# Natural context tiles loaded in three pieces of 112, 12 and 1 partitions in place of two of 112 and 13

## What is computed

```python
x = x + xattn(layernorm(x), ctx, ...)   # softmax(q k^T * scale) v, then a projection
x = x + ffn(layernorm(x), ...)          # L0: routed + shared experts, L1: 4 MoE layers, L2: top-2 experts, L3: quantised linear
```

## Time and profile before

| | us |
|---|---|
| median of 3 runs | 5644.4 |
| the runs | 5640.87, 5644.4, 5651.05 |
| profiled execution, its own time | 5660.02 |
| span in the profile | 5658.3 |

### The profile page before, as it was taken

How to read it: one execution, slowest core, us unless ns; L and a number is a source line. 1 busy time by engine, 2 the same in 40 slices (tenths; PEclk the granted TensorE clock), 3 DMA queues, 4 the chain that set the end, 5 groups by cost and what they waited for, 6 DMA issues and landing times. The chain is left out here.

```text
span 5658.3 us, 103574 instructions
## 1 busy us (share of the span) xinstructions
PE 4693.5 (83%) x32385; PEld 3818.4 (67%) x32385; DVE 3713.5 (66%) x7873; ACT 2780.5 (49%) x6184; POOL 2171.9 (38%) x1902
## 2 busy tenths in 40 slices
PE   5499999994699899899899847787799999996784
PEld 4366666663588888888888835665566666664574
DVE  4477777776566656656656546777677777775545
ACT  0277777773233333333333224455477777773341
POOL 0266666662311110110110024555466666662321
PEclk7699999996799999999999967888799999997887
DMA  7333443340100100100100020000344333420183
GB/s 244 76 83 83 89 88 86 81 88 15 38 17 21 24 20 20 24 20 20 25 20 20 4 60 0 0 0 0 72 94 88 86 82 86 89 64 23 26 180 64
DMA packets 190530, 314.67 MB, mean 56 GB/s; under 512 B 132372, under 2 KB 140870, under 8 KB 190406
## 3 DMA queue, kind: packets, MB, share of 16 engines
q1 hardware_dynamic: 186822, 294.71, 23.4%
q10 hardware_dynamic: 3584, 18.43, 0.8%
HBM read 146.07 MB, written 19.54 MB: 29 GB/s over the span
## 5 line engine op out<-in xcount | busy, mean ns | idle before, releaser
L486 POOL TENSOR_TENSOR a2m_prob_n<-a2m_prob,a2m_rec 128x500 f32<-128x500 f32 x672 | 666.6, 1020 | 377.7 <-DVE a2m_rec L671 297.1
L486 POOL TENSOR_TENSOR a0m_prob_n<-a0m_prob,a0m_rec 128x500 f32<-128x500 f32 x672 | 666.2, 1019 | 374.3 <-DVE a0m_rec L671 300.1
L1244 ACT ACTIVATE a1m_prob<-a1m_ps_s,a1m_neg_max 128x500 f32<-128x500 f32 x672 | 405.8, 675 | 557.4 <-DVE a1m_neg_max L1182 557.4
L1103 PE MATMUL a1m_ps_o<-a1m_cn,a1m_prob_t 125*128 125x97 f32 x5376 | 653.8, 280 | 0.2 <-issue 0.2
L1103 PEld LDWEIGHTS a1m_ps_o<-a1m_cn,a1m_prob_t 125*128 125x128 f32 x5376 | 641.8, 198 | 0.4 <-issue 0.4
L1033 POOL TENSOR_TENSOR a1m_cxt<-a1m_raw,g_zeros 98x1500 fp32r<-98x1500 f32 x32 | 86.8, 2711 | 1430.1 <-PE a1m_ps_s L1069 1386.2
L1179 DVE TENSOR_REDUCE a1m_bank_max<-a1m_ps_s 128x1 f32<-128x500 f32 x672 | 455.7, 679 | 145.6 <-PE a1m_ps_s L1069 144.3
L649 DVE TENSOR_REDUCE a2m_bank_max<-a2m_ps_s 128x1 f32<-128x500 f32 x672 | 416.7, 671 | 159.6 <-PE a2m_ps_s L522 159.0
L649 DVE TENSOR_REDUCE a0m_bank_max<-a0m_ps_s 128x1 f32<-128x500 f32 x672 | 416.4, 670 | 159.0 <-PE a0m_ps_s L522 158.4
L727 ACT ACTIVATE a2m_prob<-a2m_ps_s,a2m_neg_max 128x500 f32<-128x500 f32 x672 | 446.7, 676 | 60.2 <-DVE a2m_neg_max L651 55.8
L727 ACT ACTIVATE a0m_prob<-a0m_ps_s,a0m_neg_max 128x500 f32<-128x500 f32 x672 | 446.5, 676 | 60.0 <-DVE a0m_neg_max L651 55.7
(11 more groups left out here) (747 smaller groups left out, 10163.5 us busy)
## 6 DMA issues: line engine op xcount, KB each, us to landing
a0m_ks<-a0m_k_hi SPq DMA_DIRECT2D x256, 187.5 KB
a2m_ks<-a2m_k_hi SPq DMA_DIRECT2D x256, 187.5 KB
a0m_ks<-a0m_k_lo SPq DMA_DIRECT2D x128, 187.5 KB
a2m_ks<-a2m_k_lo SPq DMA_DIRECT2D x128, 187.5 KB
ctx_t<-cprep_tr ACTq DMA_DIRECT2D x32, 562.5 KB
a0m_raw<-ctx_t SPq DMA_DIRECT2D x32, 562.5 KB
a1m_raw<-ctx_t SPq DMA_DIRECT2D x32, 562.5 KB
a2m_raw<-ctx_t SPq DMA_DIRECT2D x32, 562.5 KB
```

The costliest lines, as they stand in the source:

```text
L486: pool.tensor_tensor(prob_n[:, s, at], prob[:, s, at], rec[:, s:s + 1].broadcast_to([P, BK]), ALU.mult).then_inc(scaled, 1)
L1103: m = pe.matmul(ps_o[at, 0:CO], prob_t[:, u % 2, t, at], cn[:, h, t, :], start=(t == 0), stop=(t == KT - 1))
L1244: act.activation(prob[:, s, k * BK:(k + 1) * BK], ps_s[:, k, 0:BK], ACT.Exp, bias=neg_max[:, s:s + 1]).then_inc(exped, 1)
```

## The change

`SPLIT` gets a third slice: the 13 partitions become 12 and 1. The three waits on the tile's semaphore follow the number of slices. Nothing else differs.

```diff
-SPLIT = (slice(0, 112), slice(112, NK))
+SPLIT = (slice(0, 112), slice(112, 124), slice(124, NK))
...
                 for h in range(2):
-                    pe.wait_ge(loaded[h], 32 * (i + 1))
+                    pe.wait_ge(loaded[h], 16 * len(SPLIT) * (i + 1))
...
                 for h in range(slots):
-                    sp.wait_ge(ctx_in[h], 32 * ng)
+                    sp.wait_ge(ctx_in[h], 16 * len(SPLIT) * ng)
                     sp.wait_ge(ctxt_in[h], 16 * ng)
...
                     for h in sequences(u) if first_of(u) else ():
-                        pe.wait_ge(ctx_in[h], 32 * (i + 1 + (u // nu)))
+                        pe.wait_ge(ctx_in[h], 16 * len(SPLIT) * (i + 1 + (u // nu)))
```

## The result

| | before | after |
|---|---|---|
| median, us (20 runs each) | 5643.74 | 5652.93 |
| lowest and highest run, us | 5636.28, 5651.05 | 5641.51, 5666.18 |
| span of the profiled execution, us | 5658.3 | 5640.5 |

The ratio of after to before is 1.0018, 95% interval 1.0011 to 1.0026: some 10 us slower, between 6 and 15 by the interval, and about the 0.2% up to which the prediction called it no change.

A forecast was written before the change was run, and what follows sets the result against it. Prediction: TensorE is busy about 90% of the attentions; transfers set the pace in cprep, `raw` loads delay attention 3. Terms 0 + 2 + 0 + 1.2 = +3.2 us on the 5644.4 median gave 5648, range 5637 to 5663.

The forecast's parts named there:

- Issue in cprep, costed at nothing: cprep: the added issue ends 1.0 us after the first, within the 2 us of 7 rows per engine; cost 0.
- the price for lost cover as 16 us: cprep: if the 7 rows did not cover the added issue, 32 x 0.5 = 16 us.
- TensorE's wait for the tile: cprep: a sign to look for, this wait up by as much as the stage lengthens, 0 to 9 us.
- The lone row's engine in cprep, +2 us: cprep: one engine carries 9 rows; +9 us if always last, 0 if never; a quarter of the upper end taken.
- The rival of the relieved thirteenth engine: cprep and attention 3: the thirteenth engine, now relieved, sets the landing; -9 - 1 = -10 us, 5634; chance 0.10.
- the mask row's single packet: Attention 2: the one-partition mask row went as one packet, so cprep's lone row is taken as one packet.
- Attention 3, +1.2 us with its cover of 2.1 us: Attention 3: extra packets cost 6 x 2 x 0.1 us; later `raw` issue hides under 2.1 us of queueing.
- the lower bound: Attention 3: the lone row's 12 packets go to 12 engines; the bound on the other side is 12 on one.
- The rival of the exposed issue: Attention 3: later `raw` issue is uncovered, 10 to 16 us, 13 taken; 5661 us; chance 0.12.
- Attention 1, nothing: Attention 1: the load is hidden by tens of us, so the added issues cost 0.

The follow-up runs named there:

- e5: Against the kernel before: cprep alone loads 112, 12, 1, with ScalarE's store held until SP has issued the third piece; cprep 136.9 us, ratio 0.9991.
- e3: Against the kernel before: cprep alone loads three pieces of 96, 16 and 13, without a lone row; cprep 148.1 us, ratio 1.0016.
- e9: Against the kernel before: the whole change in all three stages, with cprep's store held until the third piece is issued; cprep 137.9 us, ratio 0.9996.
- e2: Against the kernel before: the three pieces in attentions 1 and 3 alone, cprep with two; cprep 138.6 us, attention 3 227.1 us, ratio 0.9994.
- e8: Against the kernel before: attentions 1 and 3 load four pieces (112, 11, 1, 1), cprep two; attention 3 233.9 us, ratio 1.0010.
- e1: Against the kernel before: the three pieces (112, 12, 1) in cprep alone, attentions with two; cprep 147.0 us, ratio 1.0022.
- e4: Against the kernel before: cprep alone loads four pieces of 112, 11, 1 and 1; cprep 149.1 us, ratio 1.0020.
- e6: Against the kernel before: two pieces, but in cprep SP holds the 13-row piece until ScalarE has issued the store; cprep 151.5 us, ratio 1.0034.
- e7: Against the kernel before: two pieces, with cprep's store held until SP has issued both; cprep 138.2 us, ratio 0.9996.

## Why the prediction was right, and where it wasn't

The forecast was no change, 5648 us in a range of 5637 to 5663; 5653 came out. The side was right, slightly slower, by cprep. The size was +3.2 us, the measured one about +10, and the reason that I gave for the slower part isn't the one that holds: cprep grew by a mechanism that the prediction had costed at nothing, and that this still fell inside the range was partly luck.

*Issue in cprep, costed at nothing.* This is the step of the working that failed. "The piece comes last, behind 7 rows per engine" took the load's own rows as the only work in front of the piece. The tile's landing was treated as one queue's matter, and ScalarE's queue, whose stores run in the same stretch, wasn't laid beside it. The copy of the third bank and the store were in view: with 0.5 us per piece and the copy's 0.68 us, the third piece's start, 1.0 us after the first, falls behind the store. I had the price for lost cover as 16 us; it measured 7.5 us in cprep. Nor did TensorE's wait for the tile rise by as much as the stage, as the prediction said it would: it rose by 1.7 us, where the stage of the same profile grew by 6.3.

*The lone row's engine in cprep, +2 us.* Not seen. e5 has the lone row and is no slower than before, e3 has none and is as slow as the change. Whether that engine would be first or last makes no measurable difference while the pieces stand in front of the store. The rival of the relieved thirteenth engine falls with it: e5 and e9, 136.9 and 137.9 us against 138.7, show no gain of 9 us. The Trainium skill's rule of which engines a DMA takes ("DMA: Bandwidth & Descriptors", why a DMA increments its semaphore by 16) spoke against the change through this term; the packet counts agree with its number of engines, 12 for the 12 runs too, and no run here shows which engines these are, or a cost of the lowest-numbered ones. The count behind the mask row's single packet has a slip without effect: the gate load's 8 data packets are of 512 bytes and not among the 6760, which are 480 + 6144 + 8 + 128.

*Attention 3, +1.2 us with its cover of 2.1 us.* The lone row was spread, the lower bound. Nothing grew that can be told from the scatter of 2 us (e2 227.1, after 224.2 and 223.9, before 225.9 and 225.8). The cover was real and about as large as worked out: the change's 1.7 us of later issue (forecast 1.6) fit under it, and e8's 3.8 us did not, of which 1.8 came through to ScalarE's start; that made 8 us, where e8's forecast of 6 iterations of 1.7 us was 10. The rival of the exposed issue was right that issues beyond the cover come through (e8), and wrong that the change's two go beyond it or that the cover is none.

*Attention 1, nothing*: the tens of us of cover held.

*By what means the store holds the later piece back.* Two readings fit the lengths of the stages: the piece's packets start later, or they are in time and the piece's closing update waits for the store's writes. The Trainium skill says of the latter that the closing write of a DMA lands only after every earlier write of that engine, across its queues ("DMA: Bandwidth & Descriptors", the section on queues, rings and completion order). The packets of e1 speak for the first: where the last update stands apart, the last row starts 5.18 us after the first issue and the row before it at 3.94, its closing packet follows at once and the update 0.6 us later, against 0.5 in the kernel before; of a delay by that rule no run here shows more than this 0.1 us. Over all tiles that can be told apart, the last row starts at a median of 4.94 us in e1, 4.45 before and 4.46 in e5. That the late row stands behind rows of the store on its own engine is the likely reason, but it isn't shown, as the trace doesn't name a packet's engine.

What stays open is what makes up the 3 us between cprep's mean growth (138.7 to 146.2 us over two profiles each, 7.5) and the measured +10. The 7.5 lie within the interval of 6 to 15, and e9 leaves nothing for the rest. In the profiled executions of e1, e3 and e4 attention 2 is at 1118 to 1126 us, 6 us and more above every other one; after, its repeat and e6 don't have this, so it isn't put down to the pieces.

## What to carry to other kernels

Before a DMA is cut into more pieces, lay the timelines of all queues side by side and ask what another engine issues in the time that one more issue takes; the last piece's place in that order counts, not its size. Where a load that the pipeline waits for and a store that it doesn't are released by the same event, and a piece of the load would come behind the store, let the store wait for the load's last issue; it costs one semaphore per slot. Where no piece comes behind, there was nothing to gain (e7). A single profile of a 5650 us kernel can't show 10 us in its span, but it shows 7 us in a stage of 140.

## What the runs showed of the hardware that I had not expected

A load piece of 4.6 KB issued 0.3 us behind a 562.5 KB store on another queue landed late, its update a median of 0.75 us after the tile's others, and the same piece ahead of the store cost nothing (cprep 147.0 us in e1 against 136.9 in e5). What was late was the row's own packet; the closing packet and the update followed as usual. The cost is nearly blind to the piece: 1 row in e1, 13 rows in e3 and two lone rows in e4 gave 147.0, 148.1 and 149.1 us. An engine's lone extra row cost nothing measurable at a DMA share of 0.87 (e5, from 16.6 to 153.5 us); the trace doesn't say whether that engine had eight rows already.
